# The last stage of a graph network kernel: skip and down summed by TensorE, the norm applied by ScalarE

## The reference, cut to what matters

```python
out = agg.reshape(n, HID) + (x @ Wskip + bskip)
h = jax.nn.gelu(out @ W1 + b1, approximate=True)
h = jax.nn.gelu(h @ W2 + b2, approximate=True)
return out + h
...
x = _layernorm(x + _L1_gnn_ref(x, edge_index, ...), axis=-1)   # (x - m) / sqrt(v + eps)
```

## Time and profile before

| | |
|---|---|
| median of 3 runs | 6087.27 us (6085.18 to 6090.76) |
| the profiled execution | 6087.56 us |
| its span in the trace | 6085.8 us |
| first inversion of the last stage | 5293.86 us |
| last scatter begins | 6077.2 us |
| finished pairs, inversions, scatters | 198, 99, 396 |
| adds on DVE (L2822) | 198, 427 ns each |
| scales on DVE (L2853) | 396, 342 ns each |
| turns by PE (L2628) | 396, 303 ns each |

### The profile page before, as it was taken

How to read it: one execution, slowest core, us unless ns; L and a number is a source line. 1 busy time by engine, 2 the same in 40 slices (tenths; PEclk the granted TensorE clock), 3 DMA queues, 4 the chain that set the end, 5 groups by cost and what they waited for, 6 DMA issues and landing times. The chain is left out here.

```text
span 6085.8 us, 103985 instructions
## 1 busy us (share of the span) xinstructions
PE 5029.0 (83%) x26752; PEld 4077.5 (67%) x26752; DVE 4721.2 (78%) x14274; ACT 2815.7 (46%) x8831; POOL 3935.9 (65%) x3976
## 2 busy tenths in 40 slices
PE   7499999998798769966699778976698869877765
PEld 3389999997687448843488447854487658666654
DVE  8577777776687657878787886879887879888886
ACT  7167777775465653322233332333232237644442
POOL 1377777777665875556555875567666866466664
PEclk9699999998899989989899998999897569989998
DMA  0289988875466879989898998989997556444332
GB/s 2 54 230 264 262 264 260 248 246 175 149 205 191 263 241 313 322 295 345 301 322 299 320 332 289 323 317 383 319 286 214 176 150 172 143 125 124 124 120 78
DMA packets 930909, 1406.71 MB, mean 231 GB/s; under 512 B 157981, under 2 KB 453981, under 8 KB 930355
## 3 DMA queue, kind: packets, MB, share of 16 engines
q1 hardware_dynamic: 650867, 872.50, 44.6%
q0 software_dynamic: 138368, 296.57, 17.5%
q10 hardware_dynamic: 141120, 231.27, 10.1%
HBM read 827.23 MB, written 572.88 MB: 230 GB/s over the span
## 5 line engine op out<-in xcount | busy, mean ns | idle before, releaser
L1388 DVE SCALAR_TENSOR_TENSOR c_rows<-bank,carry,c_rows 32x256 f32<-32x256 f32 (+2 forms) x1950 | 889.5, 456 | 562.0 <-PE bank L1990 262.7
L1756 PE MATMUL bank<-c_rows,sums_all 128*128 128x256 f32 (+1 forms) x1960 | 736.4, 463 | 435.0 <-DVE c_rows L1388 417.6
L1396 POOL DMA_INDIRECT c_rows<-t_tab,src_pair x784 | 741.0, 945 | 519.8 <-PE bank L1990 360.6
L1396 POOL DMA_INDIRECT c_rows<-y_tab,src_pair x784 | 789.2, 1007 | 382.7 <-issue 170.5
L1756 PEld LDWEIGHTS bank<-c_rows,sums_all 128*128 128x128 f32 x1960 | 344.9, 221 | 817.4 <-DVE c_rows L1388 800.7
L1775 ACT ACTIVATE c_squares<-c_y,c_root 128x256 f32<-128x256 f32 x784 | 391.8, 500 | 803.5 <-DVE c_y L1865 392.1
L2033 ACT ACTIVATE c_xt<-bank 128x512 f32<-128x512 f32 x392 | 234.0, 597 | 905.0 <-PE bank L1999 905.0
L1753 PE MATMUL bank<-bias_rows,c_degs 128*128 128x256 f32 (+1 forms) x1960 | 621.6, 405 | 27.3 <-DMA c_degs<-kap_tab 27.3
L749 PE MATMUL bank<-w_mix,lxt 128*128 128x256 f32 x2400 | 611.2, 383 | 1.4 <-ACT lxt L1026 1.4
L749 PE MATMUL bank<-w_mix,c_xt 128*128 128x256 f32 x2352 | 606.2, 381 | 0.0
L750 PE MATMUL bank<-bias_rows,two_r 128*128 128x256 f32 (+1 forms) x1400 | 593.4, 426 | 0.0
(11 more groups left out here) (388 smaller groups left out, 12953.5 us busy)
## 6 DMA issues: line engine op xcount, KB each, us to landing
y_tab<-ly SPq DMA_DIRECT2D x400, 256.0 KB
t_tab<-lt SPq DMA_DIRECT2D x400, 256.0 KB
c_own<-y_tab SPq DMA_DIRECT2D x392, 256.0 KB
t_tab<-c_y ACTq DMA_DIRECT2D x392, 256.0 KB
c_own<-t_tab SPq DMA_DIRECT2D x392, 256.0 KB
c_z<-y_tab SPq DMA_DIRECT2D x294, 256.0 KB
y_tab<-c_y ACTq DMA_DIRECT2D x294, 256.0 KB
c_z<-t_tab SPq DMA_DIRECT2D x294, 256.0 KB
```

What stands on the lines that cost most here:

```text
L1388: nc.vector.scalar_tensor_tensor(rows, before[p0:p0 + 32, :], m["carry"][p0:p0 + 32, t:t + 1], rows, ALU.mult, ALU.add).then_inc(S["carrie ...
L1396: pool.indirect_dma_start(out=two(m["c_rows"], j % 4, H2)[:, i, 0:w], out_offset=None, in_=source, in_offset=bass.IndirectOffsetOnAxis(ap= ...
L1756: nc.tensor.matmul(out, sums[:, 2 * j + i, :], two(rows, j % 4, H2)[:, i, 0:w], start=False, stop=True).then_inc(S["summed"], 1)
```

## The change

DVE's `add` and its tile `fl_sum` go. `back` on PE, which turned the sum, now takes skip and down one after the other as the stationary operand against the identity and adds them in the accumulator: two matmul calls for each transpose call. ACT's `skip_` and `down_`, which overwrite these slots, now wait for `back`. DVE's `scale` goes; in its place one instruction makes the shift, minus mean times inverse root, for two pairs, and ACT applies scale and shift with four ACTIVATEs at the end of its turn (`apply_both`, lag 7).

```diff
@@ -2621,12 +2621,13 @@
                                      ).then_inc(S["down"], 1)
 
                 def back(j):
-                    pe.wait_ge(S["sum"], fp.at("sum", j))
+                    pe.wait_ge(S["down_set"], fp.at("down_set", j))
                     if j >= 2:
                         pe.wait_ge(S["y"], fp.at("y", j - 2))
                     for i in range(2):
-                        last = nc.tensor.transpose(psum[6 + j % 2][:, i * P:(i + 1) * P],
-                                                   both[:, j % 2, i * P:(i + 1) * P], ident[:])
+                        out_ = psum[6 + j % 2][:, i * P:(i + 1) * P]
+                        nc.tensor.matmul(out_, skip[:, j % 4, i * P:(i + 1) * P], ident[:], start=True, stop=False)
+                        last = nc.tensor.matmul(out_, down[:, j % 2, i * P:(i + 1) * P], ident[:], start=False, stop=True)
                     last.then_inc(S["back"], 1)
                 in_turns(total, [(0, 1, alpha_turn), (BEGIN + 2, every, add_up(0)), (0, each, turn), (1, each, skip_),
                                  (6, 1, pair_turn(0)), (9, 1, side_turn(0)), (10, 1, pair_turn(1)),
@@ -2655,7 +2656,7 @@
                 def skip_(j):
                     act.wait_ge(S["skip"], fp.at("skip", j))
                     if j >= 4:
-                        act.wait_ge(S["sum"], fp.at("sum", j - 4))
+                        act.wait_ge(S["back"], fp.at("back", j - 4))
                     nc.scalar.activation(skip[:, j % 4, :], psum[3][:, 0:2 * P], ACT.Identity,
                                          bias=m["b_skip"][:]).then_inc(S["skip_set"], 1)
 
@@ -2669,11 +2670,23 @@
                 def down_(j):
                     act.wait_ge(S["down"], fp.at("down", j))
                     if j >= 2:
-                        act.wait_ge(S["sum"], fp.at("sum", j - 2))
+                        act.wait_ge(S["back"], fp.at("back", j - 2))
                     nc.scalar.activation(down[:, j % 2, :], psum[5][:, 0:2 * P], ACT.Gelu_apprx_tanh,
                                          bias=m["b_down"][:]).then_inc(S["down_set"], 1)
+                def apply_both(j):
+                    if j % 2:
+                        apply(j - 1)
+                        apply(j)
+
+                def apply(j):
+                    s = j % 4
+                    act.wait_ge(S["shifted"], fp.at("shifted", j))
+                    for i in range(2):
+                        last = nc.scalar.activation(y[:, s, i, :], y[:, s, i, :], ACT.Identity,
+                                                    bias=shifts[:, s, i:i + 1], scale=inverse[:, s, i:i + 1])
+                    last.then_inc(S["done"], 1)
                 in_turns(total, [(0, each, copy), (1, 1, line_copy), (1, each, skip_), (2, each, up_), (3, each, down_),
-                                 (18, 1, weight)])
+                                 (7, each, apply_both), (18, 1, weight)])
 
             @block.vector
             def _(dve):
@@ -2815,13 +2828,6 @@
                                                den[:, s, i, :].unsqueeze(2).to_broadcast([P, HEADS, HC]), ALU.mult)
                     last.then_inc(S["shared"], 1)
 
-                def add(j):
-                    dve.wait_ge(S["down_set"], fp.at("down_set", j))
-                    if j >= 2:
-                        dve.wait_ge(S["back"], fp.at("back", j - 2))
-                    v.tensor_tensor(both[:, j % 2, :], skip[:, j % 4, :], down[:, j % 2, :], ALU.add
-                                    ).then_inc(S["sum"], 1)
-
                 def norm(j):
                     s = j % 4
                     dve.wait_ge(S["back"], fp.at("back", j))
@@ -2841,24 +2847,18 @@
                     dve.wait_ge(S["stats"], fp.at("stats", j))
                     v.tensor_scalar(var[:, s, :], mv[:, s, :, 1], LN_EPS, None, ALU.add).then_inc(S["var"], 1)
 
-                def scale_both(j):
+                def shift_both(j):
                     if j % 2:
-                        scale(j - 1)
-                        scale(j)
-
-                def scale(j):
-                    s = j % 4
-                    dve.wait_ge(S["inverse"], fp.at("inverse", j | 1))
-                    for i in range(2):
-                        last = v.tensor_scalar(y[:, s, i, :], y[:, s, i, :], mv[:, s, i, 0:1], inverse[:, s, i:i + 1],
-                                               ALU.subtract, ALU.mult)
-                    last.then_inc(S["done"], 1)
+                        dve.wait_ge(S["inverse"], fp.at("inverse", j))
+                        s = (j - 1) % 4
+                        v.scalar_tensor_tensor(shifts[:, s:s + 2, :], mv[:, s:s + 2, :, 0], -1.0,
+                                               inverse[:, s:s + 2, :], ALU.mult, ALU.mult).then_inc(S["shifted"], 2)
                 in_turns(total, [(1, 1, line_copy), (3, 1, gates), (6, 1, blocks(0)), (7, 1, to_row(0)),
                                  (9, 1, across(0)), (10, 1, within(0)), (10, 1, blocks(1)), (11, 1, to_row(1)),
                                  (13, 1, across(1)), (14, 1, within(1)), (17, 1, max_flip), (18, 1, subtract),
-                                 (BEGIN + 2, every, carry_on(0)), (7, each, scale_both),
+                                 (BEGIN + 2, every, carry_on(0)), (7, each, shift_both),
                                  (BEGIN + 5, every, divide), (6, each, norm), (BEGIN + 3, every, carry_on(1)),
-                                 (4, each, add), (BEGIN + 1, every, weigh)])
+                                 (BEGIN + 1, every, weigh)])
 
 
 # ---- launch: one core; inputs and outputs as the reference has them ----
```

More of the change, by code:

```diff
@@ L2410, in shares_and_finish @@
                             "copied": 1, "skip": 1, "skip_set": 1, "up": 1, "up_set": 1, "down": 1,
-                            "down_set": 1, "sum": 1, "back": 1, "y": 1, "stats": 2, "var": 1,
+                            "down_set": 1, "back": 1, "shifted": 1, "y": 1, "stats": 2, "var": 1,
                             "inverse": 1, "done": 1, "scattered*": 32})
@@ L2451, in shares_and_finish @@
         down = sb("fl_down", [P, 2, 2 * P])
-        both = sb("fl_sum", [P, 2, 2 * P])
+        shifts = sb("fl_shift", [P, 4, 2])
         y = sb("fl_y", [P, 4, 2, D])
```

## The result

6322.73 us median (6321.92 to 6328.66) against 6086.23: ratio 1.039, interval 1.0372 to 1.0408. The changed kernel is slower by 236 us, where 175 were forecast, and lies 13 us above the stated range. Apart from one slow execution of 10612.8 us, the kernel before took 6082.52 to 6102.63 us in twelve executions, so differences of some 15 us between single executions are read from the rounds in the traces.

A forecast was written before the change was run, and what follows sets the result against it. POOL's ring of 7.48 us, not DVE, bounds the last stage. 76 x (9.65 - 7.48) = 165, 7 for fourteen other rounds and 3 for nine late ones: 175 on 6087.27, so 6262 us; range 6125 to 6310, its own 6234 to 6305.

The forecast's parts named there:

- What bounds the kernel: Last stage: POOL's inversion, DVE's scale and POOL's scatters set rounds of 7.48 us, POOL waiting 1.44 for the scaled rows.
- The move to ACT: Norm's apply: first scatter 1.91 us after the inversion's end, against 1.44, so 0.47 per round even with ACT free.
- T0: The end of one of POOL's inversions, from which the prediction counts the times of a round.
- The faster rival: POOL's scatter start: DVE's four scales, not POOL's queue, hold it, so rounds of 7.35 and 6064 us; chance 0.06.
- The late apply and the turn-end wait: ACT's apply stands last in its turn, skip_ waits for PE's back; apply 1.7 us late, rounds of 9.28.
- The half clock: PE at 1.2 GHz: 1.86 us more in two rounds, 0.93 in one, for 4 rounds in 10; 9.28 becomes 9.65.
- The walk: Full-clock timeline over PE and ACT: 10.94 us from inversion's end to next apply, plus 7.62, so 18.56 for two rounds.
- the 76 rounds: Of 99 last-stage rounds, those having two turns with shares; forecast to go from 7.48 to 9.65 us, 165 in all.
- its last rival: Worse than the forecast: PE at half clock in every round and more waits chain, 6310 us and above; chance 0.06.
- the first six rounds: Last-stage rounds before the shares: forecast to pay only 0.47 us each, with ACT in time.
- The nine late rounds: Near the end, rounds of 11.58 us where POOL waits for a variance: forecast at some 3 us more together.
- the signs: What would show the forecast right, such as rounds of 9 to 10 us and DVE busy 60 to 65%.

The follow-up runs named there:

- b1: The kernel before with POOL's scatters two turns later, behind the next inversion, and eight slots for finished rows; 6031.90 us (6102.63 before).
- e5: The changed kernel with ACT's apply_both moved to the front of its turn, waits for back kept; 6142.68 us (6102.63 before).
- e6: The changed kernel with apply_both first in ACT's turn, eight slots for skip and four for down; 6143.77 us (6102.63 before).
- e2: The kernel before with only the norm's apply moved to ACT (shift on DVE), DVE's add and PE's transposes kept; 6225.88 us (6088.03 before).
- e1: The changed kernel with eight slots for skip and four for down, so ACT waits only for older backs; 6248.53 us (6088.03 before).
- e3: The changed kernel with DVE's scale back in place of shift and apply, waits for back kept; 6100.86 us (6088.03 before).
- e4: The changed kernel with DVE's scale back, eight slots for skip and four for down; 6100.01 us (6088.03 before).
- b5: The changed kernel with POOL's scatters two turns later and eight slots for finished rows, waits for back kept; 6087.01 us (6086.78 before).
- b2: The changed kernel with scatters two turns later, eight slots for rows, eight for skip and four for down; 6037.17 us (6086.78 before), ratio 0.9916.
- b3: The kernel before with apply on ACT, scatters two turns later, eight slots for rows, add and transposes kept; 5992.02 us (6086.78 before), ratio 0.9847.

## Why the prediction was right and where it was not

**What bounds the kernel** was right: POOL's ring of inversion, rows and scatters, not DVE. b1 takes 0.63 off the round without touching DVE's work, while the change takes a fifth of DVE's busy time per round (201.6 us in 39 rounds, 5.2 each, for 348.4 in 53.5, 6.5 each) and loses.

**The move to ACT, 0.47 per round**: the first scatter comes 1.99 behind the inversion where ACT is in time, 0.55 more than the 1.44 of the earlier trace rows, and nearly all rounds of e5 and e6 are 7.94. The 0.08 on top of the forecast is DVE starting the shift at 5758.81, 0.11 behind T0 and not 0.03. The two tiles' ACTIVATEs end at 5759.88 (four take 1.65 at 0.49, so 0.39 apart), the scatter starts at 5760.69: 0.81, as forecast.

**The faster rival** falls with that 0.81: DVE's four scales stand ahead of these scatters no more, and they start no sooner. Small `tensor_scalar` instructions do run in that gap (fl_var and w_dn, 5760.20 to 5760.46). But in 15 of the 99 rounds neither a `tensor_scalar` nor a copy of DVE does, and the gap is 0.80 there too. One of them, the first tile's rows ready at 6180.55:

```profile
6179.68 1.64 ACT L2685 ACTIVATE fl_y<-fl_y,fl_shift,fl_inv 128x128 f32<-128x128 f32 x4
...
6180.66 0.49 DVE L2841 BATCH_NORM_STATS2 fl_stats<-fl_y 128x6 f32<-128x128 f32 x2
...
6181.35 1.03 POOL L2535 DMA_INDIRECT out_dram<-fl_y,node_of  x1 [4.80 <-ACT fl_y L2685]
6181.46 0.17 DVE L2848 TENSOR_SCALAR fl_var<-fl_mv 128x2 f32<-128x2 f32 x1
```

The rule of the Trainium skill ("SBUF — State Buffer", "Who interferes with whom") that such an instruction can hold GpSimd's descriptor writes did not set this gap.

**The late apply and the turn-end wait** were right, and each is shown by itself: e2 has the one (138 us), e1 both the apply and the products without the wait (160), the change all three (236). The clock moves with them (0.86 in e1, 0.84 in e2, 0.91 in the change), so these are prices with its effect in them. The wait alone costs little while POOL's ring is the longer one (rounds of 7.52 in e3, 7.45 in e4) and 0.58 per round where it is not (7.39 in b5, 6.81 in b2). ACT is late by what its place in the turn makes it late: moved first, the loss is 40 to 50.

**The half clock is the step that failed**, by its size. I put a half-clock stretch on 4 rounds in 10 and added 0.4 x 0.93. Two chains of two rounds each are under way at any time, and I had both run at the mean. The runs show that they do not: one chain is late and the other waits, rounds alternate 7.94 and 12.55, and in the long one PE idles 4.42 and not 2.5 us. The stretch behind it runs at 0.55 of the clock (the window above), on the late chain, in every pair of rounds. The share of time at half clock was about right (0.91 over the 400 us, so 18% of 20.49, 3.7 us in two rounds: one such stretch). The price was wrong: a stretch was charged 0.93, half of what it adds to its chain, and each one costs the whole 1.86. The walk's two rounds at half clock, 18.56 + 1.86 = 20.42, measured 20.49; its chain from T0 to apply, 10.94 + 1.86 = 12.80, measured 12.86. With 0.93 in each round in place of 0.37 the 76 rounds give 76 x (10.21 - 7.48) = 207, and 214 were measured. That is the upper end of the forecast's own range (6305) and the first half of its last rival, half clock in every round, which had a chance of 0.06. The measured time lies 18 above that end: 7 more in the 76 rounds, and what follows.

**The rest**: the first six rounds cost 11 for 3, and the four behind the 76 cost 8 for 2. The forecast had ACT in time in both. In the first six e2 pays 8 as well, e5 4 and e6, with apply first and the slots, 2, so apply is late there too; what delays it, beside the scans that DVE runs for the attention's maximum, was not followed up. The nine late rounds, forecast at 3, cost 2. The products by themselves cost 13 there (e3) and the move to ACT by itself gains 4 (e2); that DVE's lighter turn pays for the products is argued from these two and not shown. Of the signs, the rounds of 10.3 lie just above 9 to 10, and DVE at 60 to 65% was wrong: 50% was measured, and the prediction's own terms give 6.5 less 0.83 less two adds of 0.34, so 5.0 of 9.65 or 52%.

## What to carry to other kernels

Ask which engine waits inside the ring that sets the pace, and what else stands in front of the moved instruction on the engine that gets it: ACT had half its time free, and its one in-order list put apply behind a whole turn of PE's work. A buffer that is freed by an engine later in the same turn turns a pipeline into a relay; that costs little while another ring is longer (e3 beside e4), and 0.6 per round once it sets the pace itself (b5 beside b2). Where a ring has a wait in it, try first to take the wait out (scatters one round later, 0.6 per round): only then did less work on DVE pay (rounds of 6.85 in b1, 6.32 in b3).

## What was not expected of the hardware

The granted clock makes up about a quarter of the loss (0.85 x 76 = 65 of 236 us): it is 0.91 over the steady rounds both before and after, but after the change its slow stretches all fall on the late chain, once in each pair of rounds behind PE's idle 4.42 us. Eight matmuls that nobody reads, 1.95 us of each round on PE, raised it to 1.00 and took 0.85 us off each round (10.30 to 9.45). In e2 the clock was 0.84 with PE idle 5.1 us ahead of a slow stretch; in e3, with PE 86% busy, it was 0.99 over the same 400 us.
